# GpSimd's addition two pieces earlier, in front of the scaled inputs, and ScalarE's weighing in slot 17, in a fused two-layer kernel

## The reference, cut to what matters

```python
xn = _layernorm(x)
x = x + attention(xn, Wq, Wk, Wv) + experts(xn, gate_w, w1, w2)   # experts: gate * expert_out[slot of the token]
xn = _layernorm(x)
x = x + mamba(xn, ...) + linear(quantise(xn), quantise(weight), bias)

# inside mamba, for 512 channels d and 16 states n
delta = softplus(dt_low @ dt_proj_w.T + dt_proj_b)
h = exp(delta * A) * h + delta * B * u        # along the tokens
y = sum_n(h * C) + u * D
```

## Time and profile before

| | before |
|---|---|
| median of 3 runs | 2026.71 us (2022.96 to 2026.82) |
| profiled execution, its own time | 2028.68 us |
| its span | 2026.9 us |
| mean granted clock of TensorE | 0.864 of full speed |
| from drive 24 of one stretch to drive 24 of the next, b = 1 to 6 | 119.40, 119.46, 119.53, 119.41, 119.45 us |

### The profile page before, as it was taken

How to read it: one execution, slowest core, us unless ns; L and a number is a source line. 1 busy time by engine, 2 the same in 40 slices (tenths; PEclk the granted TensorE clock), 3 DMA queues, 4 the chain that set the end, 5 groups by cost and what they waited for, 6 DMA issues and landing times. The chain is left out here.

```text
span 2026.9 us, 22043 instructions
## 1 busy us (share of the span) xinstructions
PE 1669.0 (82%) x6616; PEld 747.4 (37%) x6616; DVE 1511.9 (75%) x2254; ACT 998.1 (49%) x1524; POOL 892.4 (44%) x662
## 2 busy tenths in 40 slices
PE   7388999999999999999987678687886869878465
PEld 7252534536253443526233123233332323323032
DVE  6446474564646466454658999999999999999998
ACT  3115435252533435253565756656575665657542
POOL 2710000000000000000349787978788887877863
PEclk9988989899898989999879677898877788887666
DMA  5573451536364351626234232433424233341520
GB/s 192 197 117 106 78 147 43 89 108 104 105 93 131 58 121 66 105 98 107 88 110 168 104 116 95 129 118 119 145 84 157 95 125 109 119 147 54 166 94 11
DMA packets 103331, 223.83 MB, mean 110 GB/s; under 512 B 12913, under 2 KB 65266, under 8 KB 99554
## 3 DMA queue, kind: packets, MB, share of 16 engines
q1 hardware_dynamic: 100194, 214.70, 38.2%
q0 software_dynamic: 3072, 8.37, 1.3%
HBM read 169.57 MB, written 53.48 MB: 110 GB/s over the span
## 5 line engine op out<-in xcount | busy, mean ns | idle before, releaser
L1325 POOL TENSOR_TENSOR work<-rep,bc 128x1024 f32<-128x1024 f32 x256 | 596.4, 2355 | 152.8 <-PE ps L1657 144.3
L1554 DVE TENSOR_TENSOR_SCAN ps<-ps,work 128x512 f32<-128x512 f32 x512 | 624.0, 1219 | 14.1 <-POOL work L1325 8.3
L1447 ACT ACTIVATE ps<-rep,a_neg 128x512 f32<-128x512 f32 x512 | 344.9, 688 | 294.2 <-DVE work L1560 292.2
L832 DVE TENSOR_REDUCE m<-ps 128x1 f32<-128x512 f32 x512 | 328.1, 685 | 164.0 <-PE ps L967 160.4
L719 ACT ACTIVATE prob<-ps 128x1024 f32<-128x1024 f32 x256 | 257.5, 1021 | 233.2 <-PE ps L991 231.4
L1560 DVE TENSOR_TENSOR work<-ps,bc 128x512 f32<-128x512 f32 x512 | 344.2, 672 | 0.0
L637 POOL TENSOR_TENSOR m_parts<-m,nil 128x16 bf16<-128x16 f32 x32 | 7.0, 220 | 590.0 <-DVE m L832 590.0
L1632 PE MATMUL ps<-xn_sb,front_w 128*128 128x512 f32 (+1 forms) x448 | 214.4, 632 | 33.3 <-ACT xn_sb L1381 33.3
L1657 PE MATMUL ps<-work,pick 128*32 128x512 f32 x1024 | 163.5, 717 | 83.5 <-DVE work L1560 83.5
L967 PE MATMUL ps<-k_st,q_st 96*128 96x512 bf16 x512 | 202.3, 439 | 35.6 <-DVE m L832 25.4
L991 PE MATMUL ps<-q_st,k_st 99*128 99x512 bf16 x512 | 166.5, 423 | 0.9 <-DVE e_rest L808 0.4
(11 more groups left out here) (206 smaller groups left out, 2004.2 us busy)
## 6 DMA issues: line engine op xcount, KB each, us to landing
rep<-rep_rows SPq DMA_DIRECT2D x128, 512.0 KB, 6.3
front_w<-in_w SPq DMA_DIRECT2D x32, 1024.0 KB, 8.5
bc<-bc_rows SPq DMA_DIRECT2D x32, 512.0 KB, 4.7
rep_rows<-inputs SPq DMA_DIRECT2D x32, 512.0 KB, 5.4
qk_parts<-parts SPq DMA_DIRECT2D x96, 128.0 KB
q_st<-qk_parts SPq DMA_DIRECT2D x96, 128.0 KB, 10.1
k_st<-qk_parts SPq DMA_DIRECT2D x96, 128.0 KB, 11.5
dispatch<-zeros SPq DMA_DIRECT2D x4, 1280.0 KB, 10.6
```

The lines of the kernel that those rows point to most:

```text
L832: nc.vector.tensor_reduce(m[:, g % 2, qt, 2 * pair + i:2 * pair + i + 1], ps[:, S0 + i, :], AX.X, ALU.max).then_inc(s_reduced, 1)
L1325: nc.gpsimd.tensor_tensor(work[:, n % WS, :, :], rep[:, g % RS, 2 * h:2 * h + 2, 1, :], bc[:, k, 0, :].unsqueeze(1).broadcast_to([P, 2, SE ...
L1447: nc.scalar.activation(state(m), rep[:, g % RS, 2 * h + i, 0, :], ACT.Exp, scale=a_neg[:, c, 2 * h + i, k:k + 1]).then_inc(decay_ready, 1)
L1554: nc.vector.tensor_tensor_scan(state(m), state(m), work[:, n % WS, i, :], 0.0, ALU.mult, ALU.add).then_inc(state_ready, 1)
```

## The change

`weigh_experts` moves from slot 21 of ScalarE to slot 17. `add_experts` moves from slot 26 of GpSimd to slot 24. The four `scale_input` move from slots 25 to 28 to slots 26 to 29. The order on GpSimd becomes: drive 24, addition, drive 25, drive 26, c0, drive 27, c1, drive 28, c2, drive 29, c3, drives 30 and 31, root. No instruction is added or taken away.

```diff
-ACT_AT = {"weigh": -11, "normalise": -3, "turned": (0, 0), "x": (4, 6, 8, 10), "round": 5, "silu_u": 11, "quant": (12, 12), "rows": 14,
+ACT_AT = {"weigh": -15, "normalise": -3, "turned": (0, 0), "x": (4, 6, 8, 10), "round": 5, "silu_u": 11, "quant": (12, 12), "rows": 14,
           "dt": (16, 16, 18, 18), "softplus": 20, "z": (26, 27, 29, 30), "silu_z": 31}
 DVE_AT = {"max": 0, "statistics": -8}
-POOL_AT = {"gather": -16, "add": -6, "root": -1, "down": 7, "up": 10, "input": 25}
+POOL_AT = {"gather": -16, "add": -8, "root": -1, "down": 7, "up": 10, "input": 26}
```

## The result

| | before | changed |
|---|---|---|
| median | 2026.05 us (2022.9 to 2026.82, 8 runs) | 2032.27 us (2031.64 to 2035.3, 8 runs) |
| ratio | | 1.0038, 95% interval 1.0027 to 1.0049 |
| span of the profiled execution | 2026.9 us | 2029.9 us |

By the medians the change makes the kernel 6.2 us slower; the ratio of 1.0038 would be 7.7 us.

A forecast was written before the change was run, and what follows sets the result against it. VectorE's work and GpSimd's path from TensorE's tenth sum to the root were taken as the two limits. Five stretches at 1.12 us gave 5.6: 2026.71 + 5.6 = 2032.3, less perhaps 0.3, so 2032.0 us; range 2025.5 to 2035.5.

The forecast's parts named there:

- The wait at slot 24 goes, and reappears at slot 30: VectorE, b = 1 to 5: the 2.2 us statistics wait moves to slot 30, making about 3.9 us there; gain 0.
- c0 and the addition change places around the tenth sum: GpSimd, drive 26 to root: c0 (3.42 us) replaces the addition (2.30), so the root comes 1.12 us later per stretch.
- 26.8 us from drive 26 to the root: Sign on GpSimd in the profile after: this path was to take 25.7 + 1.1 = 26.8 us.
- the exchange: GpSimd ahead of the root: c0 minus the addition, 1.12 us per stretch, 0.78 as lower bound.
- Drive 26 waits 1.4 us: GpSimd in front of drive 26: earlier work ends 1.4 us before TensorE's tenth sum, so it waits that long.
- The weighing costs nothing in slot 17: ScalarE, slot 17: its 1.69 us fit into 1.96 us of waits for VectorE; cost 0, with 0.27 us to spare.
- The inputs' transfers are hidden: Scaled inputs' store and load: there near 1533.5, wanted by the next drive 0 past 1541; no cost.
- b = 0 and b = 6 cost nothing: First and last stretches: 0 in b = 0; 0 in b = 6, with a range of 0 to 1 us.
- The size: Whole kernel: five stretches, b = 1 to 5, at 1.12 us each give 5.6 us slower; predicted median 2032.0 us.
- TensorE's clock: Transposes and slot 0 projection: even at 1.2 GHz the transposes would add only 2.2 us, hidden; cost 0.
- the rival of the clock: TensorE's slot 0 projection kept at the low clock by the longer pause: 10 us more, 2042 us; chance 0.03.

The follow-up runs named there:

- its own kernel: Only the weighing moved, from slot 21 to slot 17 of ScalarE, against the kernel before: 2025.83 us, ratio 1.0003.
- addition in slot 23 and root in slot 30: Against the kernel before: weighing in slot 17, addition in slot 23, root in slot 30, inputs still from slot 25: 2008.03 us, ratio 0.9917.
- the filler: Two zero-weight TensorE matmuls behind slot 31, added to the changed kernel: 1.0037 to before; added to it with root in slot 30: 0.9961 (0.9994 without).
- the inputs alone: Only the scaled inputs moved, from slots 25 to 28 to slots 26 to 29, against the kernel before: 2044.91 us, ratio 1.0100.
- the addition in slot 23: Against the kernel before: weighing in slot 17, addition in slot 23, inputs from slot 25 and root in slot 31 unchanged: 2016.51 us, ratio 0.9956.

## Why the prediction was right, step by step

- *The wait at slot 24 goes, and reappears at slot 30.* Right: none left in the loop, and 3.2 to 4.2 us at slot 30 where 3.9 was forecast. ScalarE's wait for the root is 7.19 us, forecast 6.9.
- *c0 and the addition change places around the tenth sum.* Right, and shown by experiment from both sides: move c0 back or move the tenth sum, and the cost is gone; leave only c0 behind, and it is 19 us. The step is 34.86 - 33.80 = 1.06 us where 1.12 was forecast, with c0's idle time of 0.50 us kept in b = 1 to 5 and 0.16 in b = 6, as assumed. My 26.8 us from drive 26 to the root was too long by 0.4: I had added the exchange to b = 3, which has the extra 0.30 us ahead of c3.
- *Drive 26 waits 1.4 us.* Right: 1.44, and 1.43 or 1.44 in the others.
- *The weighing costs nothing in slot 17.* Right, by its own kernel.
- *The inputs' transfers are hidden.* Right: a further slot costs nothing.
- *b = 0 and b = 6 cost nothing.* Right for GpSimd, but the stretches aren't free of the rest, see below.
- *The size.* 5 x 1.12 = 5.6 us was forecast. Measured are 6.2 us by the medians, 7.7 by the ratio and 5.5 between the profiles. In the profiles, from the slot 0 scans of VectorE, b = 0 is 1.8 us shorter, the next five stretches together 6.45 us longer, the rest 0.8 us longer. Of the 6.45 the path from drive 24 to the root makes 5.0: four times 1.06, and 0.76 in b = 3, whose extra 0.30 us ahead of c3 is gone. The remaining 1.4, and the 0.8 at the end, lie in stretches in which the gating waits for TensorE; my sum had nothing for them. The 1.8 of b = 0 is a chance of the profiled execution after (last section); without it the profiles would differ by about 7.3. That 5.6 comes so near 6.2 is partly luck: the exchange was a little smaller than forecast, and some 2 us came from a term that I had put at nothing.
- *TensorE's clock: the step that was wrong.* I had looked at the transposes alone, taken their 1.12 us for the high clock, and written that the projection "starts 5.03 us after the last sum in either case, so that is hidden"; the clock had 3 in 100. The transposes didn't get slower:

```profile
1543.91 1.11 PE L1620 MATMUL ps<-ident_sb,xn_sb 128*128 128x128 f32 x4 [7.72 <-ACT xn_sb L1376]
```

They couldn't, since they had run at the lower level all along: in the kernel before, the granted clock is 0.50 from 1543.14 to 1544.26, over the 1.12 us of the earlier trace rows, and still 0.50 when the projection starts. At a granted clock of 1.00 four of them take 0.65 us (addition in slot 23 and root in slot 30, at 1415.76). What does change is how long the projection behind them stays at the low clock. Before, its first 8 records took 5.55 to 5.72 us in every sequence of the loop. After:

```profile
1190.25 6.26 PE L1632 MATMUL ps<-xn_sb,front_w 128*128 128x512 f32 x8 [5.03 <-ACT xn_sb L1381]
...
1311.59 5.33 PE L1632 MATMUL ps<-xn_sb,front_w 128*128 128x512 f32 x8 [5.03 <-ACT xn_sb L1381]
...
1431.63 6.74 PE L1632 MATMUL ps<-xn_sb,front_w 128*128 128x512 f32 x8 [5.03 <-ACT xn_sb L1381]
...
1673.88 5.09 PE L1632 MATMUL ps<-xn_sb,front_w 128*128 128x512 f32 x8 [5.03 <-ACT xn_sb L1381]
```

The stretches that contain them are 121.35, 120.05, 122.06 and 119.82 us long. The granted clock is 0.50 from 1431.63 to 1437.60; over the 5.33 us at 1311.59 it is 0.69 on average. Where the first 8 take more than 6.2 us VectorE waits for the sum at slot 10:

```profile
1469.02 0.69 DVE L1568 TENSOR_TENSOR sz<-ps,sz 128x512 f32<-128x512 f32 x1 [1.07 <-PE ps L1657]
```

The clock acts at a second place, which I had not looked at: the first L1674 group of the output projection, in front of the ninth sum and so of drive 24. In the two stretches with 5.33 and 6.74 us:

```profile
1378.15 2.69 PE L1674 MATMUL ps<-out_w,sz 128*128 128x256 f32 x8
...
1499.38 3.51 PE L1674 MATMUL ps<-out_w,sz 128*128 128x256 f32 x8
```

The groups behind it take 1.89 us. From the root to drive 24 the two stretches take 85.20 and 87.20 us; of the 2.00 us between them, 1.18 come at the gating of slot 10 and 0.82 in this group. Over the five stretches the group costs no more than before, 14.7 us against 14.8; it only spreads them. What remains is the gating's share.

So the rival of the clock took part, with some 2 us of the profile rather than 10, and with pluses and minuses by stretch. The Trainium skill ("TensorE: Matmul & The Clock Gate", "HAM oscillation — how this bites in real kernels") has the array fall back in a pause and start the next burst cold; the granted clocks above agree, and the filler shows what it is worth where the pause can be filled. The rival's own reason, that a longer pause keeps the projection at the low level, is not confirmed: the pause right ahead of the projection is 5.03 us in all these rows, and the pause ahead of the transposes doesn't go with the swings. In the last five sequences of the changed kernel it is 6.6 to 7.7 us. With the inputs alone it is 6.8 to 6.9 there, and the first 8 take an even 5.7 to 5.9 us; with the addition in slot 23 it is 3.4 to 4.6 us, and they swing between 5.19 and 6.68. What decides how long the clock stays low is open, and no run changed the clock alone in the changed kernel.

## What to carry to other kernels

A wait on the busiest engine is worth its length only if the next thing that this engine asks for is also ready: follow what released the wait one stage further, and compare when each path arrives. For a move inside one queue, find the gate (here a sum of TensorE) and count what lies ahead of it and behind it; work ahead of a gate is free up to the gate, and an exchange across it costs the difference of the two pieces. The idle time ahead of a gate is the place to put work: the addition one slot further forward, with the inputs back in their place, turned +0.38% into -0.44%, and with the root a slot earlier into -0.83%.

## What the runs showed of the hardware that I had not expected

**VectorE's small operation waits out one of GpSimd's.** L1535 scales 32 columns and takes 0.18 us in six of seven sequences. In the first of the kernel before it took 1.91:

```profile
1080.88 1.91 DVE L1535 TENSOR_SCALAR front_absmax<-front_absmax 128x32 f32<-128x32 f32 x1
```

```profile
1075.78 11.59 POOL L1325 TENSOR_TENSOR work<-rep,bc 128x1024 f32<-128x1024 f32 x5 [0.29 <-DMA rep<-rep_rows]
```

GpSimd's drives follow each other every 2.32 us from 1075.78, so the third starts at 1080.4 and ends at 1082.7; L1535 ends at 1082.79. After the change it starts at 1078.38, just as a drive ends, and takes 0.18:

```profile
1078.38 0.18 DVE L1535 TENSOR_SCALAR front_absmax<-front_absmax 128x32 f32<-128x32 f32 x1
```

This is the 1.8 us of b = 0, and the short one is the exception: in the profiles of all twelve other kernels the first L1535 starts while a drive runs, takes 1.57 to 2.02 us and ends within 0.15 us of the drive's end. In the six later sequences of each kernel no GpSimd operation runs beside it, and it takes 0.18 or 0.19 us. The Trainium skill ("SBUF — State Buffer", "Terms") calls the port pair of VectorE and GpSimd exclusive, held for the full instruction; the traces agree for this operation. They don't show it for every one: the reciprocal behind it (L1537), which has both sides in SBUF too, takes 0.35 us at 1082.86 beside a drive and 0.35 us at 1199.04 beside none, and the scans and reads beside the same drives keep 1.22 and 0.67 us. What makes the difference was not tried.

**The first drain behind a gather.** c0's first operation has 0.50 us of idle time ahead of it in every stretch with a gather and 0.16 in the one without, in all thirteen kernels. It moved with c0. Whether the gather causes it was not tried.
